# First layer of a four-layer image block: from stacked 128-row operands to sixteen 32x32 tiles, and attention on the rows in use

## The reference

```
x = x + L0(_gn(x))   # 3x3 Volterra convolution: 9 linear taps + 45 products of two taps
x = x + L1(_gn(x))   # 3x3 convolution, written with FFTs
x = x + L2(_gn(x))   # a recurrent cell around softmax attention, 4 heads of 8 channels
x = x + L3(_gn(x))   # Hartley transform, mode mixing, inverse transform
```

## Time and profile before

| | |
|---|---|
| time, median of 3 runs | 372.86 us (370.72 to 373.17) |
| span of the profiled execution | 369.9 us |
| layer 0, from the normalised input to the last matmul | 8.2 to 65.1 us |
| its statistics and normalisation done (layer 1 may start) | 72.6 us |
| layers 1 and the convolutions of layer 2 | up to 115.4 us |
| attention | 115.4 to 313 us |
| PE busy | 311.3 us (84%) |
| mean granted TensorE clock | 0.950 of full speed |

### The profile page before, as it was taken

How to read it: one execution, slowest core, us unless ns; L and a number is a source line. 1 busy time by engine, 2 the same in 40 slices (tenths; PEclk the granted TensorE clock), 3 DMA queues, 4 the chain that set the end, 5 groups by cost and what they waited for, 6 DMA issues and landing times.

```text
span 369.9 us, 5771 instructions
## 1 busy us (share of the span) xinstructions
PE 311.3 (84%) x2163; PEld 109.3 (30%) x2186; DVE 229.8 (62%) x494; ACT 173.0 (47%) x334; POOL 44.0 (12%) x44
## 2 busy tenths in 40 slices
PE   5599665688997556999999999999999799885994
PEld 1133111232342112333232323323232222333931
DVE  5980053834846662668786886777877221579945
ACT  2100000012335546978888787878878786300000
POOL 5000600400000000001010100101010102405100
PEclk9989966999999986999999999999999999998798
DMA  2799996000066953970000000000000000000001
GB/s 87 155 202 226 205 182 171 0 3 0 10 194 139 140 108 109 248 313 2 2 2 2 2 1 1 2 1 4 0 3 0 1 3 0 2 0 1 4 2 57
DMA packets 6283, 23.89 MB, mean 65 GB/s; under 512 B 1048, under 2 KB 1816, under 8 KB 5712
## 3 DMA queue, kind: packets, MB, share of 16 engines
q1 hardware_dynamic: 6000, 23.43, 26.3%
q0 software_dynamic: 256, 0.11, 0.2%
HBM read 11.59 MB, written 2.37 MB: 38 GB/s over the span
## 4 chain that ended last, share of the span: by engine, by line
PE 44%; DVE 10%; issue 5%; ACT 4%; another core or an unknown queue 0%; DVEq 0%; ACTq 0%
PE ps L1160 12%; PE ps L1178 12%; PE ps L1137 11%; DVE arena_a L461 3%; ACT arena_b L677 3%; PE ps L1290 2%; PE ps L1183 2%; PE ps L1233 2%; DVE mx L889 1%; PE ps L1250 1%; ACT relus L685 1%; DVE arena_a L965 1%; DVE sums L884 1%; PE ps L1298 1%; PE ps L1006 1%
## 5 line engine op out<-in xcount | busy, mean ns | idle before, releaser
L677 ACT ACTIVATE arena_b<-ps 128x512 f32<-128x512 f32 x232 | 125.2, 608 | 33.5 <-PE ps L1160 16.8
L1137 PE MATMUL ps<-arena_a 128*128 128x450 bf16 x256 | 86.1, 364 | 16.0 <-issue 11.5
L1160 PE MATMUL ps<-arena_a 128*128 128x512 bf16 x207 | 78.1, 386 | 1.0 <-ACT arena_b L677 0.4
L889 DVE TENSOR_REDUCE mx<-ps 128x1 f32<-128x450 f32 x120 | 69.2, 617 | 6.5 <-PE ps L1137 4.8
L884 DVE CUSTOM_DVE_ANT_0 sums<-ps,relus 128x450 bf16<-128x450 f32 x68 | 41.2, 625 | 40.5 <-PE ps L1137 31.1
L1178 PE MATMUL ps<-arena_b,vt 128*32 128x512 f32 x448 | 59.7, 605 | 0.7 <-ACT arena_b L677 0.7
L1160 PEld LDWEIGHTS ps<-arena_a 128*128 128x128 bf16 x224 | 21.6, 98 | 76.9 <-ACT arena_b L677 50.4
L685 ACT ACTIVATE relus<-ps 128x450 f32<-128x450 f32 x68 | 37.4, 556 | 11.0 <-PE ps L1137 10.9
L1006 PE MATMUL ps<-zeros 128*128 128x512 bf16 x109 | 29.0, 407 | 8.4 <-DMA xa<-x 3.5
L1137 PEld LDWEIGHTS ps<-arena_a 128*128 128x128 bf16 x256 | 23.8, 99 | 40.1 <-issue 10.7
L639 ACT ACTIVATE arena_b<-ps 96x386 f32<-96x386 f32 x3 | 1.5, 490 | 63.3 <-PE ps L1055 63.2
(11 more groups left out here) (131 smaller groups left out, 250.0 us busy)
## 6 DMA issues: line engine op xcount, KB each, us to landing
arena_b<-arena_a SPq DMA_DIRECT2D x12, 578.0 KB, 10.4
arena_b<-wmodes SPq DMA_DIRECT2D x1, 4096.0 KB, 22.0
arena_a<-k_scratch SPq DMA_DIRECT2D x3, 516.8 KB
arena_b<-arena_a SPq DMA_DIRECT2D x4, 306.0 KB, 5.6
arena_a<-q_scratch SPq DMA_DIRECT2D x3, 384.0 KB
arena_b<-arena_a SPq DMA_DIRECT2D x4, 272.0 KB, 5.0
k_scratch<-arena_b SPq DMA_DIRECT2D x3, 344.5 KB, 3.3
cst<-consts SPq DMA_DIRECT2D x1, 1029.0 KB, 11.1
```

Of the source, the lines that this page charges most:

```text
L677: nc.scalar.activation(probs[:, n % PRING, :], ps[:, SCORE_RING[n % len(SCORE_RING)], :], ACT.Exp).then_inc(expd, 1)
L889: nc.vector.tensor_reduce(mx[:, a, e:e + 1], bank, AX.X, ALU.max).then_inc(max_read, 1)
L1137: mm(ps[:, block_bank(i), 0:KHALF], qst[:, e, g, qt * P:(qt + 1) * P], kst[:, g, at:at + KHALF], start=True, stop=True).then_inc(max_score ...
L1160: last = mm(ps[:, bank, :], kst[:, g, t * P:(t + 1) * P], qst[:, e, g, :], start=True, stop=True)
```

## The change

Layer 0 is no longer stacked. The 20 DMAs, `stack`, its semaphores and the tile table go. `TAPS` lists the 54 features, each with its own 32x32 weights. The matmul of tap r for image b reads the 32 partitions of the image in the map (or in xp itself) and writes partition group r % 4 of PSUM bank 4 e + b, where e is the left or right half of the columns: 16 different pairs of row group and column group in turn, 54 x 4 x 2 = 432 matmuls of 32 x 32 x 512. Four partial sums per image and half are left, on the four partition groups of the bank. They are copied to SBUF (`l0_parts`: six of the eight by ACT, two by DVE), and a matmul with four stacked unit matrices (`sumsel`) adds them (`sum_parts`). The left half's sum is placed after tap 24 of the right half, and its transpose, addition and statistics follow on DVE before the right half ends.

13 maps instead of 16 are made, in two column halves and only where windows reach. The attention's matmuls contract 72 or 75 rows; the two DVE fills and POOL's fill of the queries go, and POOL writes ones on 11 partitions of the keys. The constants are loaded right behind x.

The diff, without renamed semaphores and the table of constants:

```diff
-LINEAR = None
-TILES = [
...
+HALF_COLS = W // 2
+def offsets_of(d):
+    dy, dx = d
+    return [(py, px) for py in range(3) for px in range(3) if py + dy <= 2 and 0 <= px + dx <= 2]
+PRODUCTS = [(0, 0), (0, 1), (1, 0), (1, 1), (1, -1), (0, 2), (2, 0), (1, 2), (1, -2), (2, 1), (2, -1), (2, 2), (2, -2)]
+TAPS = [(None, py, px) for py in range(3) for px in range(3)]
+TAPS += [(m, py, px) for m, d in enumerate(PRODUCTS) for py, px in offsets_of(d)]
+EARLY_TAPS = 18
+SUM_AFTER = 24
+def map_part(m, e):
+    rows, cols = zip(*offsets_of(PRODUCTS[m]))
+    last = max(cols) + HALF_COLS
+    if e == 0:
+        return min(rows), max(rows) + H, min(cols), last
+    return min(rows), max(rows) + H, last, last + HALF_COLS
...
-            sp.dma_start(cst[:, 0:N_FIRST], consts[:, 0:N_FIRST]).then_inc(first_loaded, 16)
-            def stack_tile(t, n0, n1, signal):
-                maps_ = slice(SLOTS_PER_TILE * t, SLOTS_PER_TILE * (t + 1))
-                for b in range(B):
-                    sp.dma_start(stack[:, t % 3, b, n0:n1], maps[32 * b:32 * b + 32, maps_, n0:n1]
-                                 ).then_inc(signal, 16)
...
+            sp.dma_start(cst[:, 0:N_EARLY], consts[:, 0:N_EARLY]).then_inc(early_loaded, 16)
+            sp.dma_start(cst[:, N_EARLY:N_FIRST], consts[:, N_EARLY:N_FIRST]).then_inc(first_loaded, 16)
             sp.dma_start(cst[:, N_FIRST:N_CONST], consts[:, N_FIRST:N_CONST]).then_inc(consts_loaded, 16)
...
-            nc.gpsimd.memset(arena_a[64:P, 0:q_words], 0.0).then_inc(q_filled, 1)
+            pool.wait_ge(l0_done, 2 * B)
+            nc.gpsimd.memset(kst_words[64:S_ROWS], TWO_ONES).then_inc(k_filled, 1)
...
+            for e, images in enumerate((range(B), range(2))):
+                for b in images:
+                    act.wait_ge(l0_done, e * B + b + 1)
+                    nc.scalar.activation(l0_parts[:, e, b, :], ps[:, B * e + b, :], ACT.Copy).then_inc(l0_act, 1)
...
+            for e in range(2):
+                for m in range(1, N_MAPS):
+                    nc.vector.scalar_tensor_tensor(map_box(m, e), image_box(m, e), VOLTERRA_SCALE,
+                                                   image_box(m, e, *PRODUCTS[m]), ALU.mult, ALU.mult
+                                                   ).then_inc(map_ready, 1)
...
-                nc.vector.memset(arena_a[64:P, w0:w1], TWO_ONES).then_inc(k_filled, 1)
...
+                if e == 1:
+                    for b in range(2, B):
+                        dve.wait_ge(l0_done, B + b + 1)
+                        nc.vector.tensor_copy(l0_parts[:, 1, b, :], ps[:, B + b, :]).then_inc(l0_dve, 1)
+                dve.wait_ge(l0_summed, e + 1)
...
+            pe.wait_ge(padded, 1)
+            pe.wait_ge(early_loaded, 16)
+            def sum_parts(e):
+                for b in range(B):
...
+                    last = mm(ps[32 * b:32 * b + 32, e, :], c_("sumsel"), l0_parts[:, e, b, :], start=True, stop=True)
+                last.then_inc(l0_summed, 1)
...
+                for r, (m, py, px) in enumerate(TAPS):
...
+                    if e == 1 and r == SUM_AFTER:
+                        sum_parts(0)
+                    j = r % 4
...
                     for b in range(B):
+                        rows = slice(32 * b, 32 * b + 32)
+                        image = xp if m is None else maps[:, m, :]
+                        last = mm(ps[32 * j:32 * j + 32, B * e + b, :].rearrange("p (y x) -> p y x", x=HALF_COLS),
+                                  weights[rows], window(image[rows], py, px + e * HALF_COLS, 0, H, HALF_COLS),
+                                  start=(r < 4), stop=(r >= len(TAPS) - 4), skip_group_check=True)
...
-                mm(ps[:, block_bank(i), 0:KHALF], qst[:, e, g, qt * P:(qt + 1) * P], kst[:, g, at:at + KHALF],
+                mm(ps[:, block_bank(i), 0:KHALF], qst[0:PAIR_ROWS, e, g, qt * P:(qt + 1) * P],
+                   kst[0:PAIR_ROWS, g, at:at + KHALF],
...
-                    last = mm(ps[:, bank, :], kst[:, g, t * P:(t + 1) * P], qst[:, e, g, :],
+                    last = mm(ps[:, bank, :], kst[0:S_ROWS, g, t * P:(t + 1) * P], qst[0:S_ROWS, e, g, :],
```

More of the change, by code:

```diff
@@ L52 @@
 EPS = 1e-5
-LINEAR = None
-TILES = [
-    ([(LINEAR, (0, 0)), ((0, 0), (0, 0)), ((0, 1), (0, 0)), ((1, 0), (0, 0))],
-     [(py, px) for py in range(3) for px in range(3)]),
[4 rows of a table removed]
-]
-SLOTS_PER_TILE = P // C
-N_MAPS = SLOTS_PER_TILE * len(TILES)
-PLANE = 386
[L70 to L89, removed]
+N_KEPT = 45
+PLANE = 386
+HALF_COLS = W // 2
[5 more added lines that the diff above has]
+TAPS += [(m, py, px) for m, d in enumerate(PRODUCTS) for py, px in offsets_of(d)]
+N_MAPS = len(PRODUCTS)
+EARLY_TAPS = 18
+SUM_AFTER = 24
+assert len(TAPS) == 9 + N_KEPT
+def map_part(m, e):
[4 more added lines that the diff above has]
+    return min(rows), max(rows) + H, last, last + HALF_COLS
 VOLTERRA_SCALE = float(np.float32(1.0 / np.sqrt(N_KEPT)))
@@ L219, in _place @@
     return at
-N_FIRST = _place([("l0w", len(SLOTS) * 32), ("l0bias", 1)])
+N_EARLY = _place([("l0w_early", EARLY_TAPS * 32)])
+N_FIRST = N_EARLY
+for _name, _n in [("l0w_late", (len(TAPS) - EARLY_TAPS) * 32), ("l0bias", 1), ("sumsel", 32)]:
+    CONSTS[_name] = (N_FIRST, _n)
+    N_FIRST += _n
 N_CONST = N_FIRST
@@ L327, in build @@
         map_ready = sem("map_ready")
-        tile0_top = sem("tile0_top")
-        tile_in = [sem(f"tile_in{t}") for t in range(len(TILES))]
+        early_loaded = sem("early_loaded")
         l0_done = sem("l0_done")
+        l0_act = sem("l0_act")
+        l0_dve = sem("l0_dve")
+        l0_summed = sem("l0_summed")
         l0_read = sem("l0_read")
@@ new lines, in _ @@
+            dve.wait_ge(first_loaded, 16)
+            for e in range(2):
+                half = slice(e * HALF, (e + 1) * HALF)
+                if e == 1:
[3 more added lines that the diff above has]
+                dve.wait_ge(l0_summed, e + 1)
+                nc.vector.transpose(l0t[:, half].rearrange("p (x o) -> p x o", o=32),
+                                    ps[:, e, :].rearrange("p (y x) -> p x y", x=HALF_COLS)).then_inc(l0_read, 1)
+                dve.wait_ge(l0_read, 2 * e + 1)
+                nc.vector.scalar_tensor_tensor(xb[:, half], l0t[:, half], c_("l0bias"), xa[:, half], ALU.add, ALU.add
+                                               ).then_inc(l0_read, 1)
+                dve.wait_ge(l0_read, 2 * e + 2)
+                link(nc.vector.bn_stats(stats[:, 6 * e:6 * e + 6], xb[:, half]))
@@ L769, in _ @@
+            dve.wait_ge(act_map, 2)
+            norm_from_stats(xb[:], interior(xp)).then_inc(padded, 1)
             dve.wait_ge(consts_loaded, 16)
@@ L1010, in _ @@
             keep_clock(7, 12)
-            for n in (1, 3, 5, 6):
-                pe.wait_ge(map_ready, n)
-                keep_clock(7, 5)
-            l0w = c_("l0w").rearrange("p (s o) -> p s o", o=32)
-            pe.wait_ge(first_loaded, 16)
-            for e in range(2):
-                rows = [slice(32 * b, 32 * b + 32) for b in range(B)]
-                for s, (t, (py, px)) in enumerate(SLOTS):
-                    if t == 0:
-                        if s == 0:
-                            pe.wait_ge(tile_in[0] if e else tile0_top, B * 16)
-                        for b in range(B):
-                            last = mm(ps[rows[b], e, :].rearrange("p (y x) -> p y x", x=W), l0w[:, s, :],
-                               window(stack[:, 0, b, :], py, px, 16 * e, 16, W), start=(s == 0), stop=False,
-                               skip_group_check=True)
@@ new lines, in _ @@
+            for e in range(2):
+                for r, (m, py, px) in enumerate(TAPS):
+                    if r == EARLY_TAPS and e == 0:
+                        pe.wait_ge(first_loaded, 16)
+                    if m == 0:
+                        pe.wait_ge(act_map, e + 1)
+                    elif m is not None:
+                        pe.wait_ge(map_ready, e * (N_MAPS - 1) + m)
+                    if e == 1 and r == SUM_AFTER:
+                        sum_parts(0)
+                    j = r % 4
+                    weights = c_("l0w_early")[:, 32 * r:32 * r + 32] if r < EARLY_TAPS else \
+                        c_("l0w_late")[:, 32 * (r - EARLY_TAPS):32 * (r - EARLY_TAPS) + 32]
+                    for b in range(B):
+                        rows = slice(32 * b, 32 * b + 32)
[3 more added lines that the diff above has]
+                                  start=(r < 4), stop=(r >= len(TAPS) - 4), skip_group_check=True)
+                        if r == len(TAPS) - 1:
+                            last.then_inc(l0_done, 1)
```

105 lines of the change are left out of this document (31 added, 74 removed), and 4 rows, old and new, of the table TILES.

## The result

| | before | changed |
|---|---|---|
| median time | 372.23 us (370.72 to 373.17, 4 runs) | 356.51 us (353.51 to 357.85, 4 runs) |
| ratio to before, 95% interval | | 0.9562 (0.9497 to 0.9628) |
| profiled span | 369.9 us | 355.7 us |
| layer 0's last tap ends | 65.1 | 42.6 (forecast 33.3) |
| second normalised image done | 72.60 | 52.61 (forecast 40.9) |

The forecast was 341 us, 337 to 352. The stacking's waits are gone as forecast, but only 14.2 us of 31.7 are left at the end of the span. The time was lost in four places, not in one: a late first image, the pace of the sixteen tiles, a held second image, and attention. Some executions of a kernel run over 1.5% longer than its fastest; a ratio leaves these out, a range of times holds them all.

What follows compares the result with a forecast made beforehand. Layer 0 was taken as bounded by its stacking DMAs. The right half's transpose 29.9 us earlier plus 1.8 from halved work behind it took 31.7 off the 369.9 us span; with 3.0 added, 341.2 us, range 337 to 352.

Steps and rivals of the forecast that it cites:

- What bounds, and what the DMAs cost: Layer 0: bounded by its stacking DMAs, PE waiting 3.97, 4.72 and 5.84 us for tiles; no later event absorbs the gain.
- rival F: Behind layer 0: the gain is absorbed later by a DMA that comes no earlier; some 355 to 372 us, chance 2%.
- POOL ... covered by 25 us: After layer 0: POOL's keys fill takes some 9.3 us, from 33 to 43, and delays nothing, as ACT needs the paddings later.
- They start at 8.67; the image is there at 8.2: Layer 0's start: the first twelve clock matmuls end at 8.67, with the first normalised image already there at 8.2.
- I take 23.2 ... they overlap fully: Layer 0's 432 matmuls: 27 rounds of sixteen tiles at 0.86 us each, 23.2 us, with 32.0 if rounds did not overlap.
- rival D: Layer 0's matmuls: poor overlap between rounds, up to 32.0 us instead of 23.2; kernel 346 to 350 us, chance 14%.
- Maps, sum, tail, constants: Around layer 0's matmuls: maps hide behind PE, left half's sum 1.2 us, right half's tail 1.4 + 1.05, constants no cost.
- Attention: nothing gained, nothing lost: Attention's matmuls on fewer rows: they stream the same columns and load weights equally fast, so its time stays the same.
- rival E: Attention: fewer rows cost clock, which stood at 0.99; tens of us would go, chance 1%.

Runs made afterwards that it cites:

- experiment 1: The changed kernel with POOL's two long fills moved behind the first and second normalised images, nothing else; 349.2 us, ratio 0.9378 to the kernel before.
- experiment 3: The kernel before with only the attention's matmuls cut to 72 and 75 rows, all fills kept; 376.06 us, ratio 1.0086.

## Why the prediction was wrong, point by point

- **What bounds, and what the DMAs cost:** right. All waits for tiles went, and no DMA behind absorbed the gain (rival F).
- **"POOL ... covered by 25 us":** the step that took the time out of the range, together with the next; experiment 1, with the fills moved and all else as in the change, took 349.2 us, inside 337 to 352. I asked who waits for the fill's result; nobody does. What it costs is the 3.35 - 0.81 = 2.5 us for which it holds DVE's image, and 2.3 us in layer 1, which ran its first matmuls at 1.2 GHz after PE's 3.9 us of idle time. The length of the fill itself was right (9.28 us against 9.3).
- **"They start at 8.67; the image is there at 8.2":** wrong, 10.21. I had counted POOL's fill of `xst` neither as moved nor as costing anything. It stood behind layer 0, where it ran from 65.27 to 69.00; the change drops the wait in front of it, in lines that the cut diff above leaves out:

```diff
-            pool.wait_ge(l0_done, 1)
             nc.gpsimd.memset(xst[:], 0.0).then_inc(xst_zeroed, 1)
```

  So it runs beside the first image. That is 1.5 us, and the clock fell meanwhile: the first 68 records took 3.7 us at 1.2 GHz, where experiment 1's took 2.3 at the upper level, another 1.5 us.
- **"I take 23.2 ... they overlap fully":** the largest single term, mis-sized. 864 records took 33.1 ns each, not 26.9: 5.4 us. Both bounds were named (23.2 to 32.0) and the true value, 28.6, lies inside, but I put the forecast at the lower end; rival D, with 14%, had its size. The nearest row had four tiles; with eight that still holds, with sixteen it doesn't.
- **Maps, sum, tail, constants:** the maps hid behind PE (15.15 us for 24) and no constant was waited for; the sum took 1.5 us against 1.2, the tail 2.3 against 2.5.
- **"Attention: nothing gained, nothing lost":** wrong. A matmul's duration doesn't depend on its rows: 450 columns took 0.35 us at the upper clock and 0.58 at the lower one, with 128 rows and with 72. The clock does. Against rival E I had read 0.99 for "the stage", but that window begins at 141.7. Attention begins at 115.4, and its first 26.3 us, left out, had 0.87 before the change; in the change the same stretch, 98.6 to 124.9, had 0.58:

```profile
115.40:141.70 26.30, 14.10 (x51) 0.87 0.73 127
```

  From attention's first block to the end of the span the kernel took 355.7 - 98.6 = 257.1 us, against 369.9 - 115.4 = 254.5: with the unrounded ends 2.7 us. Alone, in experiment 3, 3.2 us.

The account, in the profiled spans: second image 11.7 us later than forecast (1.5 late start, 1.5 clock, 5.4 pace, 2.5 held image, 0.8 for the sum, its ramp and the hand-over), layer 1 2.3, up to attention 0.9, attention 2.7. Together 17.6, and 31.7 - 17.6 = 14.1 of the measured 14.2 us of span. The 0.9 goes with the cold stretch from 89.0: from the third image to attention's first block, the seven kernels with such a stretch took 30.7 us, the seven without, the kernel before among them, 29.0 to 29.8. No experiment set it. With the held images and the rows cured, 344.7 us are left, 3.5 above the forecast. That is less than the 5.4 of the pace, since attention in that trace took 252.1 us, 2.3 less than before the change; why it is shorter was not tested.

What stays open is where the fixed 6.4 ns per record come from. Sixteen times 6.4 is 103 ns a record and tile, the length of one 32*32 weight load (103 ns), as if no load were hidden once all sixteen tiles take turns; with twelve tiles 12 x 38.0 - 427 = 29 ns are left and with eight 11. No run separated the load from the number of tiles. Open too is why fewer rows lower the clock: the runs show that they do, not what the chip counts.

## What to carry to other kernels

Ask of every instruction that moves what runs beside it at its new place, not only who needs its result: a POOL fill beside DVE's fp32 write of the image stopped that write until the fill ended, while DVE's maps with two operands ran on beside one. Cutting unused rows out of a matmul saved nothing in its duration and cost clock in a stage where PE is not busy all the time. Read the clock over the whole stage, its start above all, before calling it safe. With a layout that nobody has timed, forecast between the bounds and not at the good end.

## What the runs showed of the hardware that was not expected

- DVE's fp32 image of 1024 columns took 0.81 us alone and 2.92 and 3.35 us beside POOL's fills, ending 0.55 us behind them; with the order reversed POOL's fill grew from 9.28 to 9.84 us. DVE's maps, with two operands, took 15.16 us beside a fill and 15.15 without.
- Mean clock over the first 40 us of attention: 0.79 to 0.91 with 128 rows (four traces), 0.62 to 0.70 with 72 and 75 rows (nine traces), 0.70 with 96 rows in one trace.
- 32*32 tiles of 512 columns, fp32: 55 ns a record on eight tiles, 38 on twelve, 33 on sixteen, and 34 with the row group shared four times in a row.
- Small matmuls come in groups of 128, a group no sooner than 3.45 us behind the one before: 27 ns a record, with 256 columns as with 128.
